# Value products moved behind the scores on TensorE, and GpSimd's token product cut in two, in a cross-attention and mixture-of-experts kernel

## The reference, cut to what matters

```python
ln_out = _ln(hidden_states, ln_w, ln_b)
q = _fp8_linear_pertensor(ln_out, wq, wq_scale, q_in_scale)     # clip(ln_out / scale), round to 8 bits, matmul
q = _ln(q, qln_w, qln_b)                                        # norm over each head of 128
k = _ln(_fp8_linear_pertensor(ln_out, wk, ...), kln_w, kln_b)
v = _fp8_linear_pertensor(ln_out, wv, ...)
core = softmax(q k / sqrt(128)) v                               # 16 query heads, 8 key heads, per sequence of 64
xout = the same with queries qx of ln_out, keys and values of cond
catq = _div_clamp_fp8(concatenate([core, xout]), proj_smooth)
x = x + catq wproj * scale
```

## Time and profile before

| what | value |
|---|---|
| median of 3 runs | 952.84 us (952.15 to 953.67) |
| the profiled execution's own time | 953.63 us |
| its span in the trace | 951.9 us |
| PE busy | 913.4 us (96%) |
| DVE busy | 778.6 us (82%) |
| ACT busy | 703.1 us (74%) |
| POOL busy | 491.2 us (52%) |
| granted clock of PE | 0.997 of full speed |

### The profile page before, as it was taken

The page is one execution under the profiler, slowest core; times in us unless marked ns, Lnnn a source line. Parts: engine busy times, 40 slices in busy tenths (PEclk is TensorE's granted clock), DMA queues, the critical chain, the costliest instruction groups (busy, mean ns, idle before and its releaser), DMA issues.

```text
span 951.9 us, 23136 instructions
## 1 busy us (share of the span) xinstructions
PE 913.4 (96%) x8264; PEld 620.1 (65%) x8264; DVE 778.6 (82%) x1574; ACT 703.1 (74%) x1258; POOL 491.2 (52%) x495
## 2 busy tenths in 40 slices
PE   5588999999999999999999999999999999999996
PEld 3375667677677677677677677666655666666664
DVE  6789999999999999999999999987998754444443
ACT  6998888888888888888788888864656545555553
POOL 5336767566576575576675666521056513333333
PEclk9999999999999999999999999999999999999999
DMA  9934201010011001001001100314458713333323
GB/s 214 331 95 76 60 23 56 24 52 23 29 32 43 30 29 46 29 29 46 29 29 38 38 30 28 113 51 130 143 181 254 250 37 52 62 63 54 48 29 34
DMA packets 36750, 70.45 MB, mean 74 GB/s; under 512 B 3616, under 2 KB 24736, under 8 KB 36512
## 3 DMA queue, kind: packets, MB, share of 16 engines
q1 hardware_dynamic: 27184, 54.39, 18.0%
q0 software_dynamic: 9456, 14.59, 9.1%
HBM read 55.52 MB, written 18.68 MB: 78 GB/s over the span
## 4 chain that ended last, share of the span: by engine, by line
PE 79%; DVE 10%; ACT 4%; issue 3%; POOL 3%; DMA 1%; POOLq 0%; DVEq 0%; ACTq 0%
PE b_pj L350 23%; PE b_tr L369 9%; PE b_o L410 7%; PE b_sc L381 6%; PE b_pj L1366 5%; PE b_acc L453 5%; PE b_o L1401 5%; PE b_o L1493 3%; PE b_tr L1366 3%; PE b_sc L1366 3%; PE b_pt L400 3%; PE b_pj L1446 2%; PE b_pt L1390 2%; PE b_sc L1446 1%; PE b_tr L1446 1%
## 5 line engine op out<-in xcount | busy, mean ns | idle before, releaser
L725 POOL TENSOR_TENSOR rstd<-vareps,neghalf 128x4 f32<-128x4 f32 (+1 forms) x128 | 173.2, 1353 | 10.7
L718 POOL TENSOR_SCALAR vareps<-ssq,unit 128x4 f32<-128x4 f32 (+1 forms) x128 | 66.5, 519 | 210.3 <-DVE ssq L539 210.1
L350 PE MATMUL b_pj<-w_hi,xq 128*128 128x512 f16 x384 | 147.7, 385 | 1.1 <-DVE xq L707 0.9
L350 PE MATMUL b_pj<-w_lo,xq 128*128 128x512 f16 x384 | 147.1, 383 | 0.0
L465 ACT ACTIVATE sq<-b_pj 128x512 f32<-128x512 f32 x192 | 115.6, 602 | 32.7 <-PE b_pj L350 31.2
L539 DVE TENSOR_REDUCE ssq<-sq 128x4 f32<-128x512 f32 x192 | 130.3, 678 | 10.2 <-ACT sq L465 9.0
L1342 POOL DMA_INDIRECT out<-xn x39 | 60.8, 1558 | 135.6 <-ACT xn L1572 109.6
L369 PE MATMUL b_tr<-ident,nrm 128*128 128x128 f32 x768 | 120.4, 280 | 9.1 <-DVE nrm L550 4.6
L478 ACT ACTIVATE raw<-b_pj 128x512 f32<-128x512 f32 x192 | 117.2, 610 | 0.0
L369 PEld LDWEIGHTS b_tr<-ident,nrm 128*128 128x128 f32 x768 | 88.0, 141 | 44.0 <-DVE nrm L550 13.3
L550 DVE TENSOR_TENSOR nrm<-raw,rstd 128x512 f32<-128x512 f32 x128 | 107.9, 843 | 0.4
(11 more groups left out here) (329 smaller groups left out, 2218.3 us busy)
## 6 DMA issues: line engine op xcount, KB each, us to landing
nst<-in_ffw SPq DMA_DIRECT2D x40, 512.0 KB, 3.3
wload<-in_ffw SPq DMA_DIRECT2D x20, 512.0 KB
xbuf<-zero SPq DMA_DIRECT2D x13, 387.0 KB, 9.8
xn<-xbuf SPq DMA_DIRECT2D x9, 516.0 KB, 3.7
x_sb<-in_x SPq DMA_DIRECT2D x4, 512.0 KB, 13.3
wproj<-in_ctxT SPq DMA_DIRECT2D x1, 2048.0 KB, 10.2
xhl<-in_w_all SPq DMA_DIRECT2D x4, 512.0 KB, 17.0
wproj<-in_wprojT POOLq DMA_DIRECT2D x4, 512.0 KB, 5.8
```

Source lines behind the costliest of these rows:

```text
L350: last = pe.matmul(o, x, w[kind][:, k, at:at + BANK], start=(k == 0 and n_ == 0), stop=(k == KT - 1 and n_ == len(terms) - 1))
L725: pool.tensor_tensor(rstd[:, r % 2, c, :], vareps[:, r % 2, c, :], neghalf[:, 0:1].unsqueeze(2).to_broadcast(shape), ALU.pow)\
```

## The change

Three things change. PE's value products (of pass N - 1) stand directly behind the scores in each turn, no longer between the second transposes and project 2. POOL's product of a tile's tokens is made in two instructions of half the size, in two turns one after the other, and each stands between the two `pool_rstd` steps rather than behind both and behind the rows step. The counts of the semaphores are adapted to two halves: DVE's quantization waits for both. One wait is added to the very first value products: they wait until the weights, which had used the banks `b_o`, are all converted.

```diff
+            def scaled_halves(t):
+                return 4 * t if t < 2 else 2 * t + 4
...
                 after(pe, "cev_done", N)
+                if N == 0:
+                    pe.wait_ge(s["wlo_done"], len(UNITS))
...
                 act.wait_ge(s["tr_done"], t + 1)
-                after(act, "y_done", scaled(t))
+                after(act, "y_done", scaled_halves(t))
...
             def pool_token_scaled(pool, t, part):
-                if part != 1:
+                if part not in (1, 2):
                     return
-                pool.wait_ge(s["lnt_done"], KT * t + KT)
-                pool.wait_ge(s["q16_done"], scaled(t))
-                pool.tensor_tensor(y16[:, :, :, :], lnT[:, :, :].unsqueeze(2).to_broadcast([P, KT, 4, P]),
-                                   rin[:, :, :].rearrange("p j k -> p k j").unsqueeze(3).to_broadcast([P, KT, 4, P]),
+                if part == 1:
+                    pool.wait_ge(s["lnt_done"], KT * t + KT)
+                    pool.wait_ge(s["q16_done"], scaled(t))
+                j = slice(2 * part - 2, 2 * part)
+                pool.tensor_tensor(y16[:, :, j, :], lnT[:, :, :].unsqueeze(2).to_broadcast([P, KT, 2, P]),
+                                   rin[:, j, :].rearrange("p j k -> p k j").unsqueeze(3).to_broadcast([P, KT, 2, P]),
                                    ALU.mult).then_inc(s["y_done"], 1)
...
-                dve.wait_ge(s["y_done"], M + 1)
+                dve.wait_ge(s["y_done"], scaled_halves(t) + 2 if t >= 2 else M + 1)
...
                     (1, pe_scores, "scores"),
+                    (-1, pe_values, "values"),
                     (2, pe_transpose(0), "first transposes"),
                     (3, pe_project(0), "project 0"),
                     (0, pe_probT, "probT"),
                     (3, pe_project(1), "project 1"),
                     (2, pe_transpose(1), "second transposes"),
-                    (-1, pe_values, "values"),
                     (3, pe_project(2), "project 2"),
...
-                run_slots(pool, [(3, pool_rstd(0)), (3, pool_rstd(1)), (ROWS, pool_rows), (PREP, pool_token_scaled)],
+                run_slots(pool, [(3, pool_rstd(0)), (PREP, pool_token_scaled), (3, pool_rstd(1)), (ROWS, pool_rows)],
```

## The result

The changed kernel takes 973.06 us (median of 4 runs, 972.34 to 973.66), the kernel before 952.74 us beside it: a ratio of 1.021, 95% interval 1.0195 to 1.0224, so it is 20.3 us slower. The forecast was 968 us, with a range of 963 to 975 of its own, and of 961 to 976 together with rival 3.

A forecast was written before the change was run, and what follows sets the result against it. PE's own instruction list was taken to bound the steady 52 turns. Terms: +18.7 (bank wait net of changeover gain), -2.2 (halves), -1.9 (start), +0.5 (late turns) = +15.1 us, giving 968 us, range 963 to 975.

The forecast's parts named there:

- rival 3: POOL's halves do not relieve DVE, so the 2.2 and 1.5 us don't come: 972 us, chance 10%.
- step (b): Third transposes wait for ACT's second eviction of the single bank: net +0.36 us a turn, +18.7 us over 52 turns.
- (a): PE's changes of tiling form: one fewer each turn saves 0.09 us a turn.
- the unknown changeover: PE's value products directly behind scores: extra cost between nothing and 0.09 us a turn, taken as 0.
- (c): Work queued behind the third transposes: late by the net 0.36 us, nothing else stops it; third eviction in time by 0.3.
- the start: Four turns from 66.8 to 109.4 us, paced by DVE: 0.4 from changeovers and 1.5 from POOL's halves, -1.9 us.
- the stretch behind the 52 turns: Four more turns behind 583.1 us, two at PE's pace and two at DVE's: +0.5 us.
- The halves: POOL's token product in two 0.95 us halves stops holding up DVE's `nrm`: -2.2 us in steady part, 1.5 at start.
- Rival 1: Second eviction is in time, so only the gains at changes of form, halves and start remain: 944 us, chance 10%.
- Rival 2: DVE falls onto the path, delaying exponential and second eviction by a further 0.5 us in half the turns: 981 us, 6%.
- Rival 4: The stall is 0.1 to 0.2 us a turn and the gains pay for it: 953 us, chance 4%.

The follow-up runs named there:

- experiment 6: Kernel before plus POOL's halves, third transposes behind the output projection, ACT's eviction of transposed probabilities ahead of the third eviction; value products in old place: 951.21 us for 953.33.
- experiment 7: Changed kernel with third transposes behind the output projection and ACT's eviction of transposed probabilities ahead of the third eviction: 947.72 us for the kernel before's 953.33.
- experiment 4: Changed kernel with the value products between project 1 and the second transposes: 967.60 us for the kernel before's 953.24.
- experiment 8: Changed kernel with the two waits ahead of each set of transposes in the other order, eviction of the bank first: 969.58 us for the kernel before's 953.05.
- experiment 3: Changed kernel with the third transposes moved behind the output projection: 958.46 us for the kernel before's 953.24.
- experiment 5: Changed kernel with ACT's exponential moved behind the second eviction: 973.93 us for the kernel before's 953.33.
- experiment 1: Changed kernel with the value products back behind the second transposes, so only POOL's halves are new: 950.22 us for the kernel before's 953.24.
- experiment 2: Kernel before with only the value products moved behind the scores and the added wait on the weights, POOL's product whole: 974.80 us for 953.24.

## Why the prediction was right

Its sign, its mechanism and its place held, step by step. The size came out too small: +20.3 us measured for +15.1, and all but a little of the difference lies in one number of step (b) and in which executions were profiled.

*(a) The gaps.* Second transposes to the next instruction are 0.43 us in place of 0.53, and the scores to the value products take 1.09: the unknown changeover cost 0.01, near the lower bound that was taken. Experiments 6 and 7 measure the sum by itself, 0.10 us a turn. The Trainium skill's rule that a change of tiling mode drains TensorE (TensorEngine Tiling (Array Packing), "Key Properties") agrees with this: with three changes a turn in place of four, 0.10 us went. As a forecast of the time it would have had the sign wrong, since it knows nothing of the bank.

*(b) The bank.* The wait is there in all 52 turns. ACT's chain came later by exactly the distance forecast (6.49 us). One number in this step was mis-sized, "PE starts 0.05 us after the end of ACT's instruction where it waits for one": it had been read at the scores and was 0.15 at the transposes, +0.10 a turn. (So project 2 to the third transposes, forecast as 1.25 to 1.35, came out at 1.37.) The unhidden weight load was 0.03 and not 0.05 (0.47 for 0.44), -0.02. The row that the 0.05 was read from doesn't show what it was taken for: the first transposes take 0.49 us without any wait, behind scores as behind value products, and so do the second ones behind the value products in experiment 4. With these the turn is +0.43 and not +0.36, which over 52 turns is +3.6 us; the steady part grew by 20.0 us where the sum had 18.7 - 2.2 = 16.5. Experiment 8 shows that 0.09 of the 0.15 hangs on which of the two waits is written last. With the +3.6 us, and with what the start and the stretch behind the 52 turns gave (below), the sum is +18.8 us, and the spans differ by 18.7; the medians lie 1.6 us further apart.

*(c) What is queued behind.* In the changed kernel nothing more is late, as forecast, but the margins weren't the ones named. The prediction left the third eviction 0.3 us, with an upper bound for its start (2.32 us behind the second); it came 1.62 behind it and ended at 343.95, 1.0 us ahead of the scores at 344.96. The tightest place was one that the prediction didn't name: ACT's eviction of the transposed probabilities, next in its list, ended at 344.45, and the token transposes, which need that bank, started at 344.65. That is 0.20 us, hardly more than the 0.15 that the handover of a bank took. Experiments 3 and 5 ran into it, and 3, 6 and 7 into the scores.

*The halves.* Right in kind: `nrm` is never held up, and experiment 1 gives 3.0 us for 3.7, with 2.2 in the steady part as forecast. A half costs 1.04 us and not 0.95, for half the elements of a 1.90 us instruction.

*The rest.* The start gave 1.4 us for the 1.9 forecast: experiment 2 puts the halves at 1.4 of their 1.5 and the value products at nothing for 0.4; what stands behind the 52 turns 0.1 for 0.5.

*The rivals.* Rival 1 (faster, 944 us) fell, for the changed kernel as it stands: ACT's eviction ended 0.35 us behind the moment at which the third transposes were due, as worked out, and with the handover they came 0.50 late for the 0.40 forecast. Its condition, more room for the eviction, was made in experiment 7, which gave 947.7 us. Rival 2 fell: DVE's `nrm` and subtraction kept their places and POOL's roots held DVE up for 5.2 us in all, none of which reached PE in the steady part. Rival 3 fell by experiments 1 and 2, though its 972 us lies nearer to the measured time than the forecast's 968: the halves did relieve, and the handover of the bank cost what they gave. It was right that a half can hold up DVE's product of the probabilities; in the changed kernel it happened once (last section). Rival 4 fell with the 20 us.

## What to carry to other kernels

When independent work is moved in the list of the engine that sets the time, look at what it had been covering where it stood: the value products were the only thing that gave ACT time to empty the one bank that three sets of transposes share, and 0.10 us a turn of saved changeover cost 0.53 of wait. The answer can be had from two timelines of one turn: shift the chain that the moved instructions release, and compare its end with the start of whoever needs it. To keep such a gain, move other work into the gap too, and then check the next instruction in the list of the engine that was shifted.

## What the runs showed of the hardware

The order in which two waits are written ahead of one PE instruction makes 0.09 us when one of them is late: 0.15 us from the producer's end to the first matmul with the late wait second, 0.06 with it first (experiment 8). At the scores, whose late wait is first too, the weight load started 0.05 us after it. Of the 0.09, 0.06 a turn reached the steady part. What PE does in the 0.09 us, no row shows.

A POOL product of two tensors in SBUF held up a DVE product of the same kind: in the earlier trace rows `nrm` began 0.29 us behind POOL's 1.90 us product and ended 0.55 us behind its end, which is less than its own 0.68. All 14 of these products in the kernel before have this 0.55 us, whenever `nrm` began. It took up to 2.39 us in this way, and 0.70 at most in the changed kernel. A half does the same to what it meets. It met DVE's product of the probabilities once in the changed kernel, and that took 1.03 us for 0.69 and ended 0.55 us behind the half:

```profile
86.47 1.04 POOL L675 TENSOR_TENSOR y<-lnT,rin 128x512 bf16<-128x512 f32 x1
...
87.03 1.03 DVE L587 TENSOR_TENSOR prob<-prob,rc 128x512 f32<-128x512 f32 x1
```

DVE's `cat`, with one of its inputs in PSUM, kept its 0.68 us beside POOL's `nrm`, and so did POOL its 1.04 (the changed kernel, all engines in order of time):

```profile
323.00 0.68 DVE L596 TENSOR_TENSOR cat<-b_o,rsm 128x512 bf16<-128x512 f32 x1
323.02 1.04 POOL L739 TENSOR_TENSOR nrm<-raw,rstd 128x512 f32<-128x512 f32 x1
```

The Trainium skill (GPSIMD Engine Reference, "Specifications") says that GpSimd shares its SBUF interfaces with VectorE and contends with VectorE instructions that have two SBUF inputs. These rows agree.
